# Products that nothing reads, put in TensorE's waits at three places, and a first stage that begins with its values

## The chip, the core and the metric

The kernel runs on one core of one Trainium2 chip. The metric is the device time of one execution in microseconds (us). Engines are named PE (TensorE), ACT (ScalarE), DVE (VectorE), POOL (GpSimd) and SP (SyncE, which here only issues transfers).

## What is computed

Two blocks over x, 2048 tokens by 512 features, in float32:

```
xn = layernorm(x)
x  = x + attention(xn) + experts(xn)         # softmax attention, 16 heads of 32, alibi and causal mask;
                                             # one of two experts for each token (512 -> 1024 -> 512)
xn = layernorm(x)
x  = x + linear_attention(xn) + glu(xn)      # lightning_attn in chunks of 128 with a decay for each head, then
                                             #   o * sigmoid(gate), a norm over each head, and @ Wo
                                             # _bitlinear with ternary weights: sigmoid(x w1) * (x w2), then w3

# attention: qkv = xn @ Wqkv + bqkv; softmax(q k / sqrt(32) + bias) v @ Wo + bo
# the norm over a head: og * rsqrt(mean(og * og) + EPS) * norm_w
```

## The kernel before

The program is a row of stages, each a block in which every engine has its own list of instructions: `normed_qkv_stage`, `attention_stage`, `projection_stage`, `experts_stage`, `lightning_stage`, `glu_stage`. Between two stages all engines meet (L58). Inside a stage the order on an engine is the order of the code, and semaphores (`wait_ge`, `then_inc`) are all that ties the engines together. TensorE takes a wait in order: what stands behind it in its list waits too.

Products of float32 quality are made of three passes (`three_passes`, L280 to L284): each operand is split into a rounded part (`h`, a copy on ACT, `WeightSplit.hi` at L155 for weights) and a rest (`l`, a subtraction, for weights on POOL, `WeightSplit.lo` at L169, for activations on DVE). So one 128 x 512 tile of a projection is 4 x 3 = 12 matmuls of 512 columns.

**The first stage** (`normed_qkv_stage`, L405) takes 4 chunks of 512 tokens, each of 4 tiles `t` of 128. `TokenNorm` (L302) works on a chunk in this order: statistics of the four tiles on DVE (L324, L327), one square root on ACT (L333), a short chain of five operations on 128x4 elements on DVE that ends in 1/sqrt (`rsqrt_newton`, L288, counted by the semaphore `newton`), four normalising passes on DVE (L343), 16 transposes on PE (`turn`, L352), four roundings on ACT (`high`, L358) and four rests on DVE (`low`, L362). `turn` writes its bank `k` with the features `k` of all tokens, so that a rounding needs all four tiles. Then PE makes 12 tiles of products for a chunk: four of queries, four of keys, four of values, `m` from 0 to 11. In chunk 0 ACT issues the 12 loads of weight pieces (queries first, then keys, then values); DVE computes the routing's dot products of chunk 0 (`gates`, L557) before it takes the first result. Later chunks are prepared while the one before is multiplied, at steps named `STATS_AT` and the like.

**The projection** (`projection_stage`, L1219) opens with `widen(0)`: eight products that spread the inverse softmax sums over the heads' rows, for which PE waits on loads and on two reciprocals on DVE (L1344). DVE scales two halves of the attention's output by them (L1332), ACT rounds, DVE takes the rest (L1337), and then come the products (L282 to L284) with `w.woh` and `w.wol`.

**The linear attention** (`lightning_stage`) opens with the same norm chain on chunk 0, then `first_turn` (16 transposes, L2025), roundings on ACT (L2206), rests on DVE (L2303) and the products of the values. Its tail, behind the last chunk, is `spread_inverses(3)` (L2041), four normalising passes on DVE (L2286), four roundings on ACT (L2195), four rests on DVE (L2290), and `output(3)`, four tiles of products.

`widen` and the three places at which the change adds products are in these lines:

```
            pe.wait_ge(spread_in, 16)
            widen(0)
...
            pe.wait_ge(ident_in, 16)
            first_turn()
...
            spread_inverses(NCH - 1)
            output(NCH - 1)
```

## Time and profile before

| | us |
|---|---|
| runs | 1640.88, 1642.31, 1651.42 (median 1642.31) |
| the profiled execution: its time / its span | 1642.89 / 1641.1 |
| TensorE busy | 1542.0 (94%) |
| VectorE busy | 999.8 (61%) |
| GpSimd busy | 641.7 (39%) |
| ScalarE busy | 593.5 (36%) |
| first stage / attention | to 162 / to 771 |
| projection and experts / linear attention / last feed-forward | to 1072 / to 1396 / to 1641 |

The span runs from the first to the last instruction of the trace; the time of an execution has 1.8 us more around it. The granted clock of TensorE is its share of 2.4 GHz in a stretch: 1.00 is 2.4 GHz and 0.50 is 1.2 GHz. A matmul's duration overlaps with the next one's, so what a matmul costs is the distance from one start to the next.

### The profile page before, as it was taken

The numbers are of one execution on the slowest core, as the hardware profiler recorded it, in microseconds if no ns is written. First come the engines' busy times: TensorE is split into PE (matmuls) and PEld (weight loads), VectorE is DVE, ScalarE is ACT, GpSimd is POOL, SyncE is SP. The second block draws the span as 40 slices with busy tenths as digits, with TensorE's granted clock in tenths as the row PEclk, the third lists the DMA queues.
The fourth block names the chain that finished last, engine by engine and source line by source line (L and its number), as shares of the span: only waits on it lengthen the run. The fifth ranks groups of instructions, "written<-read, shape, count | busy, mean of one in ns | idle before, by whom it ended". The sixth has DMA issues, their size and how long they took to land. (4 is left out here: it accounts for less than half of the span.)

```text
span 1641.1 us, 22085 instructions
## 1 busy us (share of the span) xinstructions
PE 1542.0 (94%) x7906; PEld 1076.4 (66%) x7906; DVE 999.8 (61%) x1719; ACT 593.5 (36%) x1125; POOL 641.7 (39%) x534
## 2 busy tenths in 40 slices
PE   5999989999999999997988999969999998999998
PEld 4887545454545545543667888857777776888887
DVE  7774887887878788873545655555464455232332
ACT  3121245555545555555212222254423231222221
POOL 4100277858868786700327677633020201000000
PEclk9999799999999999999899999989999999999999
DMA  6877544544526464301762222163030231420210
GB/s 237 248 256 202 128 132 117 118 108 141 121 63 171 119 135 99 108 15 33 247 215 65 65 77 72 46 204 113 1 129 1 78 93 50 148 103 1 103 52 26
DMA packets 104443, 182.07 MB, mean 111 GB/s; under 512 B 28712, under 2 KB 45224, under 8 KB 103684
## 3 DMA queue, kind: packets, MB, share of 16 engines
q1 hardware_dynamic: 87176, 119.20, 25.2%
q0 software_dynamic: 13520, 53.85, 11.1%
q10 hardware_dynamic: 3640, 7.61, 1.3%
q8 instruction: 65, 1.06, 0.3%
q14 instruction: 42, 0.34, 0.1%
HBM read 118.62 MB, written 61.74 MB: 110 GB/s over the span
## 5 line engine op out<-in xcount | busy, mean ns | idle before, releaser
L1072 ACT ACTIVATE att_probs<-att_ring 128x512 f32<-128x512 f32 (+3 forms) x640 | 298.2, 536 | 283.5 <-DVE att_ring L1103 145.8
L1094 DVE TENSOR_REDUCE att_maxes<-att_ring 128x2 f32<-128x1024 f32 (+7 forms) x366 | 339.2, 948 | 66.3 <-PE att_ring L992 55.4
L1025 PE MATMUL att_outp<-att_probs,att_vs 128*64 128x512 f32 (+3 forms) x1280 | 271.1, 545 | 0.4 <-ACT att_att L1056 0.4
L1025 PEld LDWEIGHTS att_outp<-att_probs,att_vs 128*64 128x64 f32 x1280 | 78.3, 137 | 120.0 <-issue 68.8
L1804 DVE TENSOR_TENSOR glu_hid<-glu_sig,glu_u 128x512 f32<-128x512 f32 x44 | 30.3, 688 | 140.6 <-PE glu_u L1744 140.6
L1013 PE MATMUL att_ring<-route_wah,route_wbh 102*128 102x512 f32 (+2 forms) x320 | 105.4, 403 | 6.4 <-DVE att_maxes L1094 5.2
L992 PE MATMUL att_ring<-route_wbh,route_wah 100*128 100x512 f32 (+2 forms) x320 | 102.8, 405 | 6.9 <-DVE att_maxes L1094 4.4
L1013 PE MATMUL att_ring<-moew_wal,moew_wbl 102*128 102x512 f32 (+2 forms) x320 | 101.1, 398 | 5.2 <-DVE att_maxes L1094 5.1
L992 PE MATMUL att_ring<-moew_wbl,moew_wal 100*128 100x512 f32 (+2 forms) x320 | 96.6, 378 | 3.8 <-DVE att_maxes L1094 2.3
L1013 PEld LDWEIGHTS att_ring<-route_wah,route_wbh 102*128 102x128 f32 x320 | 54.9, 191 | 68.6 <-issue 39.1
L2413 POOL TENSOR_TENSOR lin_sig<-lin_o_copy,lin_sig 128x512 f32<-128x512 f32 x16 | 20.4, 1277 | 198.5 <-ACT lin_o_copy L2266 198.5
L1013 PEld LDWEIGHTS att_ring<-moew_wal,moew_wbl 102*128 102x128 f32 x320 | 53.6, 188 | 65.4 <-issue 31.7
L1817 POOL DMA_DIRECT2D out<-glu_y x3 | 2.4, 802 | 217.3 <-DVE glu_y L1788 217.3
L1103 DVE TENSOR_TENSOR att_ring<-att_ring,route_cst 128x128 f32<-128x128 f32 x256 | 63.4, 292 | 32.5 <-PE att_ring L1013 32.0
L992 PEld LDWEIGHTS att_ring<-route_wbh,route_wah 100*128 100x128 f32 x320 | 62.9, 204 | 26.3 <-DVE att_maxes L1094 9.2
L992 PEld LDWEIGHTS att_ring<-moew_wbl,moew_wal 100*128 100x128 f32 x320 | 59.5, 189 | 20.4 <-ACT att_probs L1072 6.2
L1613 POOL TENSOR_SCALAR moe_r<-moe_z,route_f 128x512 f32<-128x512 f32 x34 | 68.6, 2022 | 3.9 <-DVE moe_z L1538 2.6
L1743 PE MATMUL glu_u<-tail_xh,tail_up 128*128 128x512 f32 x176 | 68.6, 390 | 1.3 <-DVEq L1796 1.3
L1756 PE MATMUL glu_down<-glu_w,glu_hh 128*128 128x512 f32 x176 | 68.6, 390 | 0.4 <-DVE glu_hl L1806 0.4
L1744 PE MATMUL glu_u<-tail_xl,tail_up 128*128 128x512 f32 x176 | 68.5, 389 | 0.0
L1757 PE MATMUL glu_down<-glu_w,glu_hl 128*128 128x512 f32 x176 | 68.5, 389 | 0.0
L1743 PE MATMUL glu_u<-glu_xh,tail_up 128*128 128x512 f32 x176 | 68.5, 389 | 0.0
(294 smaller groups left out, 3451.0 us busy)
## 6 DMA issues: line engine op xcount, KB each, us to landing
att_q_raw<-in_w POOLq DMA_DIRECT2D x48, 352.0 KB, 4.0
w_ternary<-att_q_out POOLq DMA_DIRECT2D x24, 352.0 KB, 2.7
tail_up<-w_ternary SPq DMA_DIRECT2D x22, 256.0 KB, 4.6
xn<-qkv_x SPq DMA_DIRECT2D x4, 1024.0 KB, 7.4
q_hi<-qkv_hi SPq DMA_DIRECT2D x16, 256.0 KB, 3.7
q_lo<-qkv_lo SPq DMA_DIRECT2D x16, 256.0 KB, 4.5
k_hi<-qkv_hi SPq DMA_DIRECT2D x16, 256.0 KB, 2.9
k_lo<-qkv_lo SPq DMA_DIRECT2D x16, 256.0 KB, 3.9
```

The source lines that it names most:

```text
L992: last = pe.matmul(out[h][:, 0:cover], qs[par][0:SROWS, h, t * P:(t + 1) * P], ks[par][0:SROWS, h, g * CH:g * CH + cover], start=True, sto ...
L1013: last = pe.matmul(out[h][:, start:CH], ks[par][:, h, kt * P:(kt + 1) * P], qs[par][:, h, c * CH + start:(c + 1) * CH], start=True, stop=True)
L1025: last = pe.matmul(outp[v_cols(h), off:CH], vs[p % 2][:, kt, v_cols(h)], probs[:, g % 4, h, off:CH], start=kt == 0, stop=kt == TT * (c + 1 ...
L1072: act.activation(probs[:, g % 4, h, off:CH], ring[:, rg.banks["score", g][h], off:CH], ACT.Exp).then_inc(exped, 1)
L1094: last = dve.tensor_reduce(maxes[:, hs, t, g:g + 1], banks[:, :, 0:width], AX.X, ALU.max)
L1103: dve.tensor_tensor(block, block, neg_k, ALU.add).then_inc(masked, 1)
L1613: pool.tensor_scalar(r[:, half, :], z[:, half, :], 0.0, rt.f1[:, j:j + 1], ALU.max, ALU.mult).then_inc(relued, 1)
L1743: pe.matmul(u[:, n % 2, :], w[:, f, k, :], xh[c % 2][:, k, :], start=k == 0, stop=False)
L1744: last = pe.matmul(u[:, n % 2, :], w[:, f, k, :], xl[c % 2][:, k, :], start=False, stop=k == KT - 1)
L1756: pe.matmul(down[:, t, :], hh[:, n % 2, s], w3[:, f, :], start=f == 0, stop=False)
L1757: last = pe.matmul(down[:, t, :], hl[:, n % 2, s], w3[:, f, :], start=False, stop=f == GT - 1)
L1804: dve.tensor_tensor(hid[:, n % 2, :], sig[:, n % 2, :], u2[:, n % 2, :], ALU.mult).then_inc(hid_ready, 1)
```

## The change

- A helper `keep_warm` issues `n` matmuls of 512 columns whose result nothing reads. It stands in TensorE's list at three places: 18 before and 6 behind `widen(0)` of the projection, 28 before `first_turn` of the linear attention, and 16 behind the last `spread_inverses`, before the last `output`. They wait for nothing, except the 16, which wait for `o` to be read (`o_taken`).
- In the first stage chunk 0 makes its values first, then queries and keys (`FIRST`). Its transposes go to a bank for each tile instead of each feature block, so that roundings, rests and the value products go tile by tile (`part`, `rows`, `xl_ready` counted one by one).
- The value weights are loaded first, on ACT's queue; the other eight pieces go to SP's queue, behind x and the constants. ACT first runs a square root on one element (`warm`).
- GpSimd waits for the first norm's short chain (`newton`) before its first rest of a weight.
- On DVE the routing's dot products are spread one to a step; two casts of constants come behind chunk 0. The second chunk's statistics, norm, transposes and roundings of chunk 0's loop get steps of their own. On SP the load of chunk `c + 2` comes behind the stores of the queries.
- `ranks` and `places` in the attention wait for both of their ring's banks instead of the first.

The core of the diff:

```diff
+def keep_warm(pe, out, wh, xh, n):
+
+    for _ in range(n):
+        pe.matmul(out, wh, xh, start=True, stop=True)
...
-                ins = pe.transpose(self.out[:, k, t * P:(t + 1) * P], self.x[c % 2][:, t, k * P:(k + 1) * P], self.ident)
-                if t == TT - 1:
+                to = (t, k) if c == 0 else (k, t)
+                ins = pe.transpose(self.out[:, to[0], to[1] * P:(to[1] + 1) * P], self.x[c % 2][:, t, k * P:(k + 1) * P], self.ident)
+                if k == KT - 1 if c == 0 else t == TT - 1:
                     ins.then_inc(self.turned, 1)
...
+    def rows(self, c, i):
+        return self.out[:, i, :].rearrange("p (k n) -> p k n", n=P) if c == 0 else self.out[:, i, :]
+
+    def high(self, act, c, i):
+        act.wait_ge(self.turned, c * KT + i + 1)
+        act.activation(self.part(self.xh[c % 2], c, i), self.rows(c, i), ACT.Copy).then_inc(self.xh_ready, 1)
+
+    def low(self, dve, c, i):
+        dve.wait_ge(self.xh_ready, c * KT + i + 1)
+        dve.tensor_tensor(self.part(self.xl[c % 2], c, i), self.rows(c, i),
+                          self.part(self.xh[c % 2], c, i).bitcast(F32), ALU.subtract).then_inc(self.xl_ready, 1)
...
+    FIRST = [*range(NQK, NP), *range(NQK)]
+    STATS_FIRST, NORM_FIRST, TURN_FIRST, HIGH_FIRST, LOW_FIRST = 2, 4, 6, 3, 7
...
-        ws = WeightSplit(st, D, [(w_d[k * P:(k + 1) * P, s], wh[:, k, s], wl[:, k, s]) for s, k in thirds[:2 * KT]]
-                         + [(w_d[k * P:(k + 1) * P, s], carried.h[:, k, :], carried.l[:, k, :]) for s, k in thirds[2 * KT:]],
-                         len(thirds))
+        ws = WeightSplit(st, D, [(w_d[k * P:(k + 1) * P, s], carried.h[:, k, :], carried.l[:, k, :]) for s, k in thirds[2 * KT:]]
+                         + [(w_d[k * P:(k + 1) * P, s], wh[:, k, s], wl[:, k, s]) for s, k in thirds[:2 * KT]], len(thirds))
...
+            for j in range(KT, len(ws.pieces)):
+                ws.load(sp, j)
...
-                if c + 2 < NCH:
-                    load_x(c + 2)
                 for m in range(NQK):
+                    if m == KT and c + 2 < NCH:
+                        load_x(c + 2)
...
-                pe.wait_ge(norm.xl_ready, (c + 1) * KT)
-                for m in range(NP):
-                    n = c * NP + m
-                    if c == 0 and m % KT == 0:
-                        ws.wait(pe, m + KT)
+                if c:
+                    pe.wait_ge(norm.xl_ready, (c + 1) * KT)
+                for i, m in enumerate(FIRST if c == 0 else range(NP)):
+                    n = c * NP + i
+                    if c == 0 and i < TT:
+                        pe.wait_ge(norm.xl_ready, i + 1)
+                    if c == 0 and i % KT == 0:
+                        ws.wait(pe, i + KT)
                     if n >= 4:
...
-                    if c + 1 < NCH and m == TURN_AT:
+                    if c + 1 < NCH and i == (TURN_AT if c else TURN_FIRST):
                         norm.turn(pe, c + 1)
...
-            ws.load_all(act)
             act.wait_ge(eps_set, 1)
-            ws.hi(act, 0)
-            ws.hi(act, 1)
+            act.activation(warm[:], eps[:], ACT.Sqrt)
+            for j in range(KT):
+                ws.load(act, j)
             norm.take_root(act, 0)
-            ws.hi(act, 2)
-            ws.hi(act, 3)
+            for j in range(KT):
+                ws.hi(act, j)
             xn_high(0)
             for j in range(KT, len(ws.pieces)):
                 ws.hi(act, j)
+            norm.take_root(act, 1)
             for c in range(NCH):
                 for m in range(NQK):
...
+            for i, m in enumerate(FIRST):
+                dve.wait_ge(made, i + 1)
+                if i < TT:
+                    value(0, i)
+                else:
+                    whole(0, m)
+                if i == STATS_FIRST:
+                    norm.stats(dve, 1, chunk_in(1))
+                if i == NORM_FIRST:
+                    norm.normalize(dve, 1)
+                if LOW_FIRST <= i < LOW_FIRST + KT:
+                    norm.low(dve, 1, i - LOW_FIRST)
+                if i == NP - 1:
+                    low(NQK - 1)
+                if NORM_FIRST < i <= NORM_FIRST + TT:
+                    gate(i - NORM_FIRST - 1)
             dve.wait_ge(ident_in, 16)
             for i, t in enumerate((early.ident, early.neg_q)):
                 dve.tensor_copy(t[:], early.cst[:, i, :]).then_inc(bf_ready, 1)
...
+            pool.wait_ge(norm.newton, norm.LINKS)
             ws.lo_all(pool)
...
                     if g == RANKS_AT:
-                        wait_freed(("ranks", 0), 0)
+                        for h in range(2):
+                            wait_freed(("ranks", 0), h)
                         router.ranks(pe)
                     if g == PLACES_AT:
-                        wait_freed(("places", 0), 0)
+                        for h in range(2):
+                            wait_freed(("places", 0), h)
                         router.sum_places(pe)
                     score(g)
...
+            keep_warm(pe, acc[:, 3, :], w.woh[:, 0, 0:P], w.woh[:, 1, :], 18)
             pe.wait_ge(spread_in, 16)
             widen(0)
+            keep_warm(pe, acc[:, 3, :], w.woh[:, 0, 0:P], w.woh[:, 1, :], 6)
             for n in range(NHC):
...
+            keep_warm(pe, o[:], carried.h[:, 0, 0:P], carried.h[:, 1, :], 28)
             pe.wait_ge(ident_in, 16)
             first_turn()
...
             spread_inverses(NCH - 1)
+            pe.wait_ge(o_taken, NCH * TT)
+            keep_warm(pe, o[:], wh["o"][:, 0, 0:P], wh["o"][:, 1, :], 16)
             output(NCH - 1)
```

ACT at the start of the first stage, its list before (the roundings of weights are L155, the square root is L333):

```order
L146 DMA qkv_wstage<-in_Wqkv 128x512 x12
L155 ACT_TABLE_LOAD
L155 ACTIVATE qkv_wh<-qkv_wstage 128x512 x2
L333 ACT_TABLE_LOAD
L333 ACTIVATE qkv_ln_root<-qkv_ln_mv,qkv_eps 128x4
L155 ACTIVATE qkv_wh<-qkv_wstage 128x512 x2
```

and now:

```order
L538 ACT_TABLE_LOAD
L538 ACTIVATE qkv_warm<-qkv_eps 128x1
L146 DMA qkv_wstage<-in_Wqkv 128x512 x4
L339 ACTIVATE qkv_ln_root<-qkv_ln_mv,qkv_eps 128x4
L155 ACTIVATE carried_h<-qkv_wstage 128x512 x4
```

The table for the square root is loaded ahead of the statistics, once; 4 loads instead of 12 stand ahead of it, and the pieces are those of the values (`carried_h`).

TensorE at the start of the projection, before:

```order
L1286 MATMUL proj_wide<-proj_inv,proj_spread 128x256 x4
L282 MATMUL proj_acc<-carried_h,proj_ath 128x512
L283 MATMUL proj_acc<-carried_l,proj_ath 128x512
L284 MATMUL proj_acc<-carried_h,proj_atl 128x512
```

and now:

```order
L283 MATMUL proj_acc<-carried_h 128x512 x18
L1332 MATMUL proj_wide<-proj_inv,proj_spread 128x256 x4
L283 MATMUL proj_acc<-carried_h 128x512 x6
L288 MATMUL proj_acc<-carried_h,proj_ath 128x512
L289 MATMUL proj_acc<-carried_l,proj_ath 128x512
L290 MATMUL proj_acc<-carried_h,proj_atl 128x512
```

The unread products stand on both sides of `widen(0)`; everything behind them in the list is as it was.

TensorE in the linear attention's tail, now:

```order
L2089 MATMUL lin_wide<-lin_inv,lin_cst 128x512 x4
L283 MATMUL lin_o<-lin_woh 128x512 x16
L288 MATMUL lin_ring<-lin_woh,tail_up 128x512
```

Before, the row in the middle was not there.

## Rows read from the trace of the kernel before

**Rows 1.** The page's busy line of TensorE (busy us, share of the span, instructions).

```profile
PE 1542.0 (94%) x7906; PEld 1076.4 (66%) x7906; DVE 999.8 (61%) x1719; ACT 593.5 (36%) x1125; POOL 641.7 (39%) x534
```

**Rows 2.** TensorE's waits (engine, line, waited for: us, times, longest).

```profile
PE qkv_turned L352 <- DVE qkv_x L343: 15.0, 1, 15.0
```

**Rows 3.** Timeline of the first stage (start, us, engine, line, operation, count, idle before).

```profile
8.56 0.69 DVE L324 BATCH_NORM_STATS2 qkv_ln_halves<-qkv_x 128x6 f32<-128x512 f32 x1 [0.65 <-DMA qkv_x<-in_x]
...
9.13 2.48 POOL L169 TENSOR_TENSOR qkv_wl<-qkv_wstage,qkv_wh 128x512 fp32r<-128x512 f32 x2 [8.70 <-ACT qkv_wh L155]
...
9.58 1.28 ACT L333 ACT_TABLE_LOAD   x1
...
11.87 1.19 DVE L298 TENSOR_SCALAR qkv_ln_tmp<-qkv_ln_tmp 128x4 f32<-128x4 f32 x1
...
14.31 1.92 DVE L343 TENSOR_SCALAR qkv_x<-qkv_x,qkv_ln_mv,qkv_ln_inv 128x512 f32<-128x512 f32 x4
...
21.21 0.79 PE L282 MATMUL qkv_acc<-route_wah,qkv_wh 128*128 128x512 f32 x1 [2.57 <-DVE route_wbh L362]
...
26.84 1.54 DVE L557 CUSTOM_DVE_ANT_0 qkv_product<-qkv_x,qkv_wg 128x512 f32<-128x512 f32 x1
...
27.35 0.44 PE L284 MATMUL qkv_acc<-route_wah,qkv_wl 128*128 128x512 f32 x1
...
43.92 0.68 DVE L557 CUSTOM_DVE_ANT_0 qkv_product<-qkv_x,qkv_wg 128x512 f32<-128x512 f32 x1
```

**Rows 4.** TensorE before the projection (window, us, busy, count, clock, DMA share, GB/s).

```profile
774.00:775.00 1.00, 0.00 (x0) 0.98 0.00 0
```

**Rows 5.** Timeline of the projection's start.

```profile
774.49 0.34 ACTq L1310 DMA_DIRECT2D proj_spread<-in_spread_heads  x1
...
779.40 3.37 DVE L1344 RECIPROCAL proj_inv<-proj_inv 128x256 f32<-128x256 f32 x2 [4.22 <-DMA proj_inv<-softmax_sums]
...
781.30 3.75 PE L1286 MATMUL proj_wide<-proj_inv,proj_spread 16*128 16x256 f32 x8 [10.29 <-DVE proj_inv L1344]
...
783.45 0.69 DVE L1332 TENSOR_TENSOR proj_at<-proj_at,proj_wide 128x512 f32<-128x512 f32 x1 [0.69 <-PE proj_wide L1286]
...
786.43 0.80 PE L282 MATMUL proj_acc<-carried_h,proj_ath 128*128 128x512 f32 x1 [1.38 <-DVE proj_atl L1337]
...
791.85 2.06 PE L1286 MATMUL proj_wide<-proj_inv,proj_spread 16*128 16x256 f32 x8
...
793.83 0.50 PE L282 MATMUL proj_acc<-carried_h,proj_ath 128*128 128x512 f32 x1
...
796.84 1.99 PE L1286 MATMUL proj_wide<-proj_inv,proj_spread 16*128 16x256 f32 x8
```

**Rows 6.** Timeline of the linear attention's start.

```profile
1076.52 1.28 ACT L2216 ACT_TABLE_LOAD   x1 [10.38 <-PEq L58]
...
1084.02 0.28 ACT L333 ACTIVATE lin_ln_root<-lin_ln_mv,lin_eps 128x4 f32<-128x4 f32 x1
...
1085.34 1.91 DVE L343 TENSOR_SCALAR tail_y<-tail_y,lin_ln_mv,lin_ln_inv 128x512 f32<-128x512 f32 x4
...
1086.03 3.37 PE L2025 MATMUL lin_wide<-lin_cst,tail_y 128*128 128x128 f32 x16 [13.70 <-DVE tail_y L343]
...
1087.78 0.69 DVE L2303 TENSOR_TENSOR tail_xl<-lin_wide,tail_xh 128x512 fp32r<-128x512 f32 x1 [0.53 <-ACT tail_xh L2206]
...
1089.15 0.47 PE L282 MATMUL lin_ring<-carried_h,tail_xh 128*128 128x512 f32 x1
```

**Rows 7.** Timeline of the linear attention's tail.

```profile
1375.06 1.14 PE L2041 MATMUL lin_wide<-lin_inv,lin_cst 32*128 32x512 f32 x8 [1.05 <-DVE lin_inv L299]
...
1381.45 0.79 PE L282 MATMUL lin_ring<-lin_woh,tail_up 128*128 128x512 f32 x1 [5.25 <-DVE lin_ogl L2290]
...
1385.88 0.43 PE L283 MATMUL lin_ring<-lin_wol,tail_up 128*128 128x512 f32 x1
```

**Rows 8.** TensorE in that tail (columns as in rows 4).

```profile
1379.00:1380.00 1.00, 0.00 (x0) 0.56 1.02 381
```

More of the change, by code:

```diff
@@ L562, in _ @@
             norm.normalize(dve, 0)
-            for k in range(KT):
-                norm.low(dve, 0, k)
+            for i in range(TT):
+                norm.low(dve, 0, i)
+            dve.wait_ge(wg_in, 16)
+            dve.tensor_tensor(wg[:, 0, :], wg[:, 0, :], wg[:, 1, :], ALU.subtract).then_inc(wg_ready, 1)
+            dve.wait_ge(wg_ready, 1)
+            dve.wait_ge(b_in, 32)
+            for i, m in enumerate(FIRST):
[14 more added lines that the diff above has]
+                    gate(i - NORM_FIRST - 1)
             dve.wait_ge(ident_in, 16)
@@ L567, in _ @@
                 dve.tensor_copy(t[:], early.cst[:, i, :]).then_inc(bf_ready, 1)
[L568 to L573 removed]
+            for c in range(1, NCH):
                 for m in range(NP):
```

76 lines of the change are left out of this document (34 added, 42 removed).

## The prediction

> **What bounds the kernel now.** I read the page first: TensorE is busy 94% of the span [rows 1], so the kernel is as long as TensorE's list plus the stretches in which TensorE stands still or runs at its lower clock. Next its waits: the longest single one is at the very start, 15.0 us until the first normalised tile [rows 2]. Then the timelines at the four places that the change touches, where "idle before" shows 10.29 us ahead of `widen(0)` [rows 5], 13.70 us ahead of the linear attention's transposes [rows 6] and 5.25 us ahead of the last output [rows 7]. The windows show what follows such a wait. TensorE ends the attention at 771.0, and its granted clock is 0.98 in the stretch from 774 and half behind it [rows 4]; in the tail it is idle from 1376.2 and the clock is 0.56 in the stretch from 1379, so half from about 1379.1 [rows 8]. The timeline gives the price: at 1.2 GHz the 12 matmuls of a tile take 791.85 - 786.43 = 5.42 us [rows 5], one each 0.43; at 2.4 GHz they take 796.84 - 793.83 = 3.01, one each 0.23 once they run. After each of these places TensorE runs without a gap worth counting, so what the place gives up moves everything behind it.
>
> **A, the first stage.** Before, ACT loads a table at 9.58 for the root that the statistics have just made possible, and DVE's normalising begins at 14.31 [rows 3]: 4.73 us. The same chain in the linear attention, with its table there already and GpSimd idle, goes from the root at 1084.02 to normalising at 1085.34, in 1.32 [rows 6]. The first stage pays the table (1.28) and about 2 us in short DVE operations held up beside GpSimd's rests: the one at 11.87 takes 1.19 us on 128x4 elements. The change takes the table load out and holds GpSimd back until the short chain is done: normalising begins at 9.58 + 1.32 = 10.9, 3.4 earlier. But now GpSimd starts just then, and its first four rests (2.48 for two, so 1.24 each) lie beside the four normalising passes. No row shows those passes beside GpSimd. The nearest is the routing's dot product: 1.54 beside GpSimd at 26.84 and 0.68 alone at 43.92 [rows 3], 0.86 more; the short operation lost 1.0. So the passes take 1.92 + 4 x 0.9 = 5.5 instead of 1.92 and end at 16.4. Behind them only the last tile's four transposes (a quarter of 3.37, 0.84 [rows 6]) and the first rest (0.69) stand, side by side, since the first product needs tile 0 alone: it starts at 17.2. The value weights' rests end at about 10.9 + 4 x 1.24 plus what the passes hold them up, 16 to 17, just in time. Before, the first product started at 21.21: **4.0 us gained**. The bounds: if each pass waits for one whole rest, a pair takes 1.24 + 0.48 and the start is at 10.9 + 6.9 + 0.8 = 18.6, a gain of 2.6. If they do not disturb each other the weights decide, at 15.9, a gain of 5.3; and if x arrives sooner, because ACT's queue has four loads ahead of the root instead of twelve, the statistics lose their waits on loads, three of about 0.6 (the last one 0.65 at 8.56), which makes 7.1. I take the row in between.
>
> Behind the start nothing should give it back. The products of chunk 0 are as many as before, and cold for some 6 us as before (21.21 to 27.35 [rows 3]). The query weights are due 12 x 4 matmuls later, over 11 us, which covers four roundings on ACT and four rests of at most 1.7. The dot products move from before the first result to beside later ones, 0.68 each, where a step of TensorE is 2.7 long; one step can have 0.74 + 0.68 + 0.69 + 0.68, about that length, and four accumulator banks absorb it. SP's load of a chunk waits one half loop longer and still has four steps. All this I cost at 0; if the cover fails, the second chunk's transposes are late next, by a step of DVE, 1 to 3 us. The second bank's wait at `ranks` and `places` is for results read two or more scores earlier: 0, at most 1 us.
>
> **B, the projection.** The 18 products start when the stage does, 774.5 (ACT's first transfer is at 774.49 [rows 5]), about where the clock falls. If it falls, they run cold until it rises; the stage itself needed 5.4 us of products for that (786.43 to 791.85). That is 13 products, and 5 warm ones take 1.2: done at 781.1, and `widen(0)` started at 781.30. So it is not held up. Warm, its eight products take 2.06 instead of 3.75 [rows 5], and DVE's scaling is no longer waited for by PE's half (783.45) but by the second reciprocal, 779.40 + 3.37 = 782.8; two scalings and a rest of 0.7 each end at 784.9, so the first product comes at 784.9 instead of 786.43: 1.5. The 6 products (1.4 us) fit into that wait. The first tile takes 3.0 instead of 5.4: 2.4. **3.9 us gained.** Bounds: 0 if the clock is down again when the tile starts; 4.5 if more of the scaling is brought forward.
>
> **C, the linear attention.** 28 products from about 1076.6 (ACT starts at 1076.52 [rows 6]): 5.4 us cold for 13, then 15 at 0.23, done at 1085.5, ahead of the transposes at 1086.03. These run warm, but they also wait for the last normalised tile at 1085.34 + 1.91 = 1087.25, and the first product waits for a rest that ends at 1087.78 + 0.69 = 1088.5, which ACT's earlier work sets. Before it started at 1089.15, warm already. **0.65 gained**, between -1 and 0.7.
>
> **D, the tail.** The 16 products start at 1376.2 behind `spread_inverses` and end at 1379.9; idle until the last rest at 1381.45 are 1.5 us instead of 5.25. The clock should stay. Before, the first ten distances took 1385.88 - 1381.45 = 4.43 [rows 7]; at 0.23 they take 2.3. **2.1 gained**, between 0 and 2.2. The 16 wait for `o_taken`, met long before.
>
> **The sum** is 4.0 + 3.9 + 0.65 + 2.1 = 10.6 us. The profiled execution took 1642.9, 0.6 above the median of the three runs (1642.3); from the median the forecast is 1631.7, so **1632 us**.
>
> **A rule weighed against this.** The 1.19 and 1.54 beside GpSimd show that the two engines hold each other up on some operations, and an excess of 0.9 to 1.0, less than a whole rest of 1.24, is what I used. The Trainium skill, "SBUF — State Buffer", section "Who interferes with whom", says that a VectorE instruction in a two-port mode, or with two inputs in SBUF, and a GpSimd instruction shut each other out for the whole instruction, so that which comes first decides. By this rule every pass can wait for a whole rest, which is the lower bound of A and the first rival.
>
> **The rivals.**
> 1. *GpSimd's rests take the place of the wait removed.* Released by the end of the short chain, they meet the normalising passes, each of which then waits a whole rest. For it: the rests are now due exactly there. Against it: an excess of 0.86 in the nearest row. A gives 2.6 or, with late value weights, less: 1633 to 1636, I say 1634. Chance 0.2.
> 2. *The start is freer than I think*: loads earlier and no mutual delay, A gives 6 to 7: 1629. Chance 0.13.
> 3. *The clock falls in spite of the products*, in the 1.5 us between the 16 and the last output, or between `widen(0)` and the first tile. For it: 1.14 us of `spread_inverses` did not hold the clock in the tail. D gives 0 and B 1.5 less: 1635 to 1638, I say 1636. Chance 0.12.
> 4. *The products stand in the way* (slower). TensorE's list is in order, so `widen(0)` waits for the 18 and the transposes for the 28. If the clock does not rise under them, 18 x 0.43 end at 782.2, 0.9 late, `widen(0)` stays cold and the 6 add 2.6 where 2.1 us of wait were: about 1.5 lost; the 28 end at 1088.6, 2.6 lost. With 4.1 lost here, nothing in D and A at 2.6 the sum is 1.5 to the bad: 1644. It decides from about 7 us of cold products on. Against it: every rise in the trace came within 6.2 us of dense work. Chance 0.03.
>
> The Trainium skill, "TensorE: Matmul & The Clock Gate", section "What's actually happening", says that the number of cold products before the rise differs from run to run of one kernel. This trace has 5.4 and 6.1 us, and in the linear attention 3.1 us of transposes (1086.03 to 1089.15) [rows 6]: that moves A's cold stretch by up to 1.5 us and the end of the 18 by as much.
>
> **From cases to numbers.** Forecast 0.5 (1630 to 1634), rivals 0.2, 0.13, 0.12, 0.03, and 0.02 for what I do not see. All gains at their upper bound make 7.1 + 4.5 + 0.7 + 2.2 + 1.5 = 16, against which nothing is likely to be complete: 1627 is the low end. Rival 3 with A at 2.6 makes 1637.5; with 1 us for the attention's waits, 1639 is the high end. A measurement of this kernel tells about 1%, 16.4 us, from no change: faster by more than that needs every upper bound, 0.04; slower by more needs something unforeseen, 0.02; within 1% 0.94.
>
> **What would show it.** In the trace after: no table load just ahead of the first root; normalising from about 10.9, its four passes longer than 1.92 together; the first product near 17. At the projection the first tile at 0.23 a matmul and `widen(0)` not later than before; clock 1.00 through the first tile. First products of the linear attention 12 us behind its stage's start instead of 12.6. In the tail the last output's first ten distances in 2.3. I am wrong if the first product starts after 19, if `widen(0)` or the transposes start at the end of unread products, or if the stages between, equal in their lists, change by more than 2 us.

## The result and the profile after

The changed kernel takes 1633.35 us, the median of 12 runs (1627.99 to 1640.89); the kernel before, beside it, 1644.68 us (12 runs, 1640.78 to 1651.42). The ratio is 0.9937, 95% interval 0.9922 to 0.9953: 11.3 us less by the medians, where 1632 was forecast. The profiled execution took 1632.59 us, its span is 1630.8 us against 1641.1.

The page's busy line of the changed kernel stands against [rows 1]:

```profile
PE 1555.3 (95%) x7974; PEld 1086.1 (67%) x7974; DVE 996.0 (61%) x1719; ACT 591.9 (36%) x1125; POOL 640.8 (39%) x534
```

TensorE is busy 13.3 us longer and yet the span is shorter. The 68 more instructions are the unread products, so busy time here is no measure of work: only the timelines tell what was won.

The span, cut at ten points that both kernels have, and the same cuts of a second trace of the changed kernel (the run `e11_changed_again` below), in us:

| stretch | before | forecast | after | again |
|---|---|---|---|---|
| start to first product | 21.2 | 17.2 | 18.2 | 17.5 |
| first product to the attention | 142.7 | 142.7 | 140.9 | 140.2 |
| attention | 610.6 | 610.6 | 609.6 | 609.9 |
| projection: start to second tile | 17.4 | 13.5 | 15.0 | 13.7 |
| rest of the projection | 59.0 | 59.0 | 58.7 | 60.6 |
| experts | 225.7 | 225.7 | 226.7 | 225.8 |
| linear attention: start to first product | 12.6 | 12.0 | 11.9 | 11.9 |
| its middle | 285.9 | 285.9 | 285.9 | 287.6 |
| its tail: inverses to the next block | 21.1 | 19.0 | 19.1 | 19.1 |
| the rest | 244.9 | 244.9 | 244.9 | 244.9 |

**First stage.** The timeline of the changed kernel (columns as in [rows 3], to which these rows answer; line 339 is the root, 349 the normalising passes, 359 the transposes, 169 a rest of a weight, 288 to 290 the three matmuls of a product), and then TensorE behind it:

```profile
0.72 1.28 ACT L538 ACT_TABLE_LOAD   x1 [0.72 <-PEq L2554]
...
9.20 0.69 DVE L330 BATCH_NORM_STATS2 qkv_ln_halves<-qkv_x 128x6 f32<-128x512 f32 x1 [0.66 <-DMA qkv_x<-in_x]
...
10.20 0.30 ACT L339 ACTIVATE qkv_ln_root<-qkv_ln_mv,qkv_eps 128x4 f32<-128x4 f32 x1 [7.98 <-DVE qkv_ln_mv L333]
...
11.54 5.82 DVE L349 TENSOR_SCALAR qkv_x<-qkv_x,qkv_ln_mv,qkv_ln_inv 128x512 f32<-128x512 f32 x4
11.59 5.49 POOL L169 TENSOR_TENSOR carried_l<-qkv_wstage,carried_h 128x512 fp32r<-128x512 f32 x4 [11.15 <-ACT carried_h L155]
...
13.28 1.09 PE L359 MATMUL qkv_turned<-route_cst,qkv_x 128*128 128x128 f32 x4 [13.28 <-DVE qkv_x L349]
...
17.41 1.11 PE L359 MATMUL qkv_turned<-route_cst,qkv_x 128*128 128x128 f32 x4 [0.29 <-DVE qkv_x L349]
```

```profile
18.18 0.77 PE L288 MATMUL qkv_acc<-carried_h,route_wah 128*128 128x512 f32 x1
...
20.88 0.41 PE L288 MATMUL qkv_acc<-carried_h,route_wah 128*128 128x512 f32 x1
```

The table load stands at 0.72, in nobody's way. The short chain takes from 10.53 to 11.54, 1.0 us. Then the four passes take 5.82 us where they took 1.92, ending some 1.4 us apart, side by side with the four rests, 1.37 each. The transposes follow pass by pass instead of all at once. The products are at full speed from 20.88: 2.7 us of cold products, where there were 6.1 [rows 3].

**Projection**, against [rows 5] (line 283 is an unread product, 1332 `widen`):

```profile
768.68 5.82 PE L283 MATMUL proj_acc<-carried_h 128*128 128x512 f32 x18 [3.53 <-PEq L58]
775.83 1.96 PE L1332 MATMUL proj_wide<-proj_inv,proj_spread 16*128 16x256 f32 x8 [1.33 <-DVE proj_inv L1392]
777.72 2.16 PE L283 MATMUL proj_acc<-carried_h 128*128 128x512 f32 x6
779.68 0.63 PE L288 MATMUL proj_acc<-carried_h,proj_ath 128*128 128x512 f32 x1
...
782.16 0.39 PE L288 MATMUL proj_acc<-carried_h,proj_ath 128*128 128x512 f32 x1
...
783.65 1.99 PE L1332 MATMUL proj_wide<-proj_inv,proj_spread 16*128 16x256 f32 x8
```

TensorE in the two microseconds around the first tile's start (window, us; then busy us and count of PE, PEld, DVE, ACT and POOL; then clock, DMA share, GB/s):

```profile
778.00:779.00 1.00, 1.00 (x5) 0.77 (x5) 0.98 (x2) 0.96 (x2) 0.00 (x0) 0.83 1.00 344
779.00:780.00 1.00, 1.00 (x4) 0.78 (x3) 0.91 (x2) 0.19 (x1) 0.00 (x0) 0.50 1.08 426
```

`widen(0)` takes 1.96 us instead of 3.75: the clock was up. Then it falls, at about 778.7, under the six unread products. Of the tile's twelve products the first five are followed by the next one 0.43 us later (a clock of 0.50), the sixth by 0.35, the others by 0.23.

**Linear attention**, its start against [rows 6]:

```profile
1068.96 1.28 ACT L2267 ACT_TABLE_LOAD   x1 [10.41 <-PEq L58]
...
1069.00 8.09 PE L283 MATMUL lin_o<-carried_h 128*128 128x512 f32 x28 [4.25 <-PEq L58]
...
1078.48 1.94 PE L2073 MATMUL lin_wide<-lin_cst,tail_y 128*128 128x128 f32 x16 [1.40 <-DVE tail_y L349]
...
1080.90 0.50 PE L288 MATMUL lin_ring<-carried_h,tail_xh 128*128 128x512 f32 x1 [0.47 <-DVE tail_xl L2354]
```

and its tail against [rows 7]:

```profile
1366.80 1.14 PE L2089 MATMUL lin_wide<-lin_inv,lin_cst 32*128 32x512 f32 x8 [1.05 <-DVE lin_inv L305]
...
1367.87 3.94 PE L283 MATMUL lin_o<-lin_woh 128*128 128x512 f32 x16
...
1373.19 0.50 PE L288 MATMUL lin_ring<-lin_woh,tail_up 128*128 128x512 f32 x1 [1.38 <-DVE lin_ogl L2341]
```

The 28 end 1.4 us before the transposes, the 16 end 1.38 us before the last output, and that output is warm from its first product. The granted clock over that tail, the third number from the end (columns as in the window lines above):

```profile
1366.00:1377.00 11.00, 8.82 (x40) 6.36 (x41) 7.71 (x13) 2.50 (x4) 0.00 (x0) 1.00 0.25 95
```

It is 1.00 where it fell to 0.56 in [rows 8].

### The profile page after: what moved, and what is told of

It is laid out like the page before. It is cut to its first block and busy times, and to the rows that moved or that the text cites. A ratio compares the mean times of both kernels' runs of the same rounds, so it can differ in the third digit from the quotient of the medians.

```text
span 1630.8 us, 22220 instructions
## 1 busy us (share of the span) xinstructions
PE 1555.3 (95%) x7974; PEld 1086.1 (67%) x7974; DVE 996.0 (61%) x1719; ACT 591.9 (36%) x1125; POOL 640.8 (39%) x534
```

## The experiments

Each run is held against runs of the kernel before on the same chip. The stretches that an edit leaves alone differ from trace to trace all the same: over the fourteen traces of this case the attention took 605.2 to 614.0 us with the same real products in it. A comparison of medians is therefore coarse (the 95% intervals below are 0.4% to 0.9% wide, 7 to 14 us), a trace tells the stretch in which an edit stands, and the verdicts below go by stretches.

### The two halves apart

`e1_products_only` is the kernel before with the unread products alone (the diff of `keep_warm` and its four calls); `e2_stage_only` is the changed kernel without them:

```diff
-            keep_warm(pe, acc[:, 3, :], w.woh[:, 0, 0:P], w.woh[:, 1, :], 18)
-            keep_warm(pe, acc[:, 3, :], w.woh[:, 0, 0:P], w.woh[:, 1, :], 6)
-            keep_warm(pe, o[:], carried.h[:, 0, 0:P], carried.h[:, 1, :], 28)
-            pe.wait_ge(o_taken, NCH * TT)
-            keep_warm(pe, o[:], wh["o"][:, 0, 0:P], wh["o"][:, 1, :], 16)
```

> The kernel before with only the unread products added, at the three places (18 and 6, 28, 16); the first stage is as before. My theory: each place works by itself. Against the kernel before: the first tile of the projection takes 3.0 to 4.0 us instead of 5.42, the first product of the linear attention comes 12.0 us behind its stage's start instead of 12.63, the last output 2.0 us sooner; in all 5 to 6.5 us less, ratio 0.996 to 0.997. Rival, that nearly all of the gain is the first stage's: ratio 0.999 or more. Rival, that the first stage hides it: ratio 0.994 as with the whole change.

> The change without any unread product. My theory: first product at 18.2 us instead of 21.2, its stage 4 to 5 us shorter in all, and nothing else; the projection's first tile takes 5.4 us again, the linear attention's first product comes 12.6 us behind the stage's start and the last output's first ten distances take 4.4 us. Ratio 0.997. Rival, that the first stage does nothing behind its own start: ratio 0.999 or more.

The products alone: 1640.59 us, ratio 0.9952 (0.9931 to 0.9974). The stage alone: 1638.57 us, ratio 0.9957 (0.9932 to 0.9983). The product of the two is 0.9909, the whole 0.9937 (0.9922 to 0.9953); with these intervals they may add up, and nothing shows that one half feeds the other. In the traces each gain stands where its half is: the first product at 21.2 and 17.5; the linear attention's start 11.9 and 12.8; its last stretch 19.1 and 21.9. Both intervals hold the ratios expected, 0.996 to 0.997 and 0.997. With the stage alone the first tile of the projection took 4.8 us instead of 5.4, with nothing changed there. The projection to its second tile took 16.3 us with the products alone, 1.1 less than before and 1.3 more than in the changed kernel, with the same 18 and 6. TensorE there:

```profile
774.95 4.36 PE L283 MATMUL proj_acc<-carried_h 128*128 128x512 f32 x18 [3.51 <-PEq L58]
781.84 2.28 PE L1292 MATMUL proj_wide<-proj_inv,proj_spread 16*128 16x256 f32 x8 [2.53 <-DVE proj_inv L1352]
...
786.77 0.63 PE L288 MATMUL proj_acc<-carried_h,proj_ath 128*128 128x512 f32 x1
```

The 18 ran at full speed, 4.36 us, and left 2.53 us of idle; `widen(0)` was partly cold and so were eight products of the tile, which took 4.4 us where 3.0 to 4.0 was expected.

### Where GpSimd's rests go

`e3_no_hold` lets GpSimd start as before, as soon as a weight is rounded; `e4_hold_longer` holds it until all four passes are over:

```diff
 e3   -            pool.wait_ge(norm.newton, norm.LINKS)
 e4   -            pool.wait_ge(norm.newton, norm.LINKS)
 e4   +            pool.wait_ge(norm.normed, TT)
```

> The change with GpSimd's wait for the short norm chain taken out, so that its rests begin as soon as ACT has rounded the first value weight (10.9 us). If holding GpSimd back matters as I reckoned, the short chain, which now takes 1.0 us from 10.53, meets one or two rests and loses 1 to 2 us, and the first product comes at 19.2 to 20 instead of 18.2. If the chain is over before it can be hit (ACT rounds only behind the root), nothing moves: 18.2 within 0.5.

> The change with GpSimd held until all four normalising passes are done instead of until the short chain is. If the passes are long because of GpSimd's rests, their 5.82 us fall to 1.92 and they end at 13.5; the rests then run from 13.5 and, no longer stretched, take 5.0 instead of 5.49, so the value weights are ready at 18.5 and the first product comes at 18.5 to 18.8, 0.3 to 0.6 later than now. If the passes are long for another reason (the tiles in use by a store, the load of chunk 1), they stay above 4 us and the first product comes at 22 or later.

Measured: 1634.65 us, 0.9922 (0.9898 to 0.9947), and 1635.85 us, 0.9935 (0.9909 to 0.9960): no difference from the whole change. The timelines of the first stage, of `e3` and then of `e4`:

```profile
10.81 5.12 POOL L169 TENSOR_TENSOR carried_l<-qkv_wstage,carried_h 128x512 fp32r<-128x512 f32 x4 [10.38 <-ACT carried_h L155]
10.84 1.25 DVE L304 TENSOR_SCALAR qkv_ln_tmp<-qkv_ln_tmp 128x4 f32<-128x4 f32 x1
...
13.35 3.77 DVE L349 TENSOR_SCALAR qkv_x<-qkv_x,qkv_ln_mv,qkv_ln_inv 128x512 f32<-128x512 f32 x4
```

```profile
10.87 1.92 DVE L349 TENSOR_SCALAR qkv_x<-qkv_x,qkv_ln_mv,qkv_ln_inv 128x512 f32<-128x512 f32 x4
...
12.87 5.42 POOL L169 TENSOR_TENSOR carried_l<-qkv_wstage,carried_h 128x512 fp32r<-128x512 f32 x4 [12.44 <-DVE qkv_x L349]
...
18.43 0.77 PE L288 MATMUL qkv_acc<-carried_h,route_wah 128*128 128x512 f32 x1 [3.23 <-POOL carried_l L169]
```

Without the hold, the meeting is only shifted: two operations of the short chain take 1.25 and 1.18 instead of 0.17 and 0.16, the passes, beside which fewer rests are left, 3.77. The first product is at 18.7. With the longer hold chain and passes are free (1.92), the rests of x come at 13.31 to 16.6, beside the weights' rests and at 0.69 each undisturbed; but the rests of the value weights end at 18.29, and TensorE waits 3.23 us for them. First product 18.4, in the range expected. x lands at another time in each run, so the fair measure is from the last statistics (9.20 in the changed kernel, 8.90, 8.53; 8.53 in its repeat) to the first product: 9.0 us in the changed kernel and in its repeat, 9.8 in `e3`, 9.9 in `e4`, 12.7 before. So the hold as the change has it is worth 0.9 us against none (less than the 1 to 2 expected), and more of it nothing: in `e3` and in the changed kernel TensorE's transposes come last, behind the passes, in `e4` GpSimd's 5.42 us. The price was shifted among them.

### Taking the bound apart

`e5_piece_waits` is `e4` with TensorE waiting for the value weights piece by piece in its first tile. `e6_early_rests` adds two roundings before the root, whose rests GpSimd makes at once:

```diff
 e5   +                        if n == 0:
 e5   +                            ws.wait(pe, k + 1)
 e6   +            ws.hi(act, 0)
 e6   +            ws.hi(act, 1)
              norm.take_root(act, 0)
 e6   -            for j in range(KT):
 e6   -                ws.hi(act, j)
 e6   +            ws.hi(act, 2)
 e6   +            ws.hi(act, 3)
 e6   +            for j in range(2):
 e6   +                ws.lo(pool, j)
              pool.wait_ge(norm.normed, TT)
 e6   +            for j in range(2, len(ws.pieces)):
 e6   +                ws.lo(pool, j)
```

> In the kernel of the run before (GpSimd held until all four normalising passes are over) TensorE waited for the rests of all the value weights, 18.3 us, before its first product. Here its first tile waits for them piece by piece, four pieces. Theory 1 (the wait for the whole is what sets the first product): the pieces are done at about 14.2, 15.6, 16.9 and 18.3 us, the first product is at about 15.3 us, where the transposes free it, instead of 18.4, and the stage ends 2 to 3 us sooner. Rival (the last piece sets the end of the first tile all the same): the first product is sooner, but the first tile ends less than 1 us sooner, and so does the stage.

> As the run with the waits piece by piece, and ScalarE rounds two of the four value pieces before the square root, and GpSimd makes their rests at once; only the other two wait for the normalising passes. Theory: the first two rests fall before the short chain, the last is done at about 15.6 us, and the first product is at about 15.2 us, bound by the transposes; the stage ends up to 1 us sooner than in the run with the piece waits alone. Rival (VectorE and GpSimd get in each other's way again): the early rests, 1.3 us each, stretch the short chain and the statistics by 1 to 2 us, and the passes, the transposes and the first product come that much later, so that the time is the same or up to 1 us worse.

TensorE in the first stage of `e5`, then GpSimd and TensorE in that of `e6`:

```profile
14.91 0.78 PE L288 MATMUL qkv_acc<-carried_h,route_wah 128*128 128x512 f32 x1
...
18.43 0.50 PE L288 MATMUL qkv_acc<-carried_h,route_wah 128*128 128x512 f32 x1 [0.58 <-POOL carried_l L169]
```

```profile
5.11 2.61 POOL L169 TENSOR_TENSOR carried_l<-qkv_wstage,carried_h 128x512 fp32r<-128x512 f32 x2 [4.68 <-ACT carried_h L155]
...
15.04 0.78 PE L288 MATMUL qkv_acc<-carried_h,route_wah 128*128 128x512 f32 x1
```

`e5`: first product at 14.9, 6.3 us behind the last statistics where it was 9.9 in `e4`, and the attention starts at 156.9 instead of 160.4: the theory, by half a microsecond more than expected. The last piece still costs 0.58 us of wait at 18.43. `e6`: that wait is gone, the attention starts at 155.3, 1.6 us earlier again, where up to 1 was expected. The wait is 0.6 of it; another 0.7 is a wait of TensorE for a later chunk's rests on VectorE, which stands at 86.9 in `e5` and not in `e6`, and which neither edit touches. Its early rests lie at 5.11 to 7.72, where VectorE waits for x, and neither the statistics nor the short chain are longer for them, so the rival is refuted. The medians, 1630.37 (0.9930, 0.9904 to 0.9956) and 1630.38 (0.9915, 0.9890 to 0.9941), don't tell the two apart: the attention of `e6` took 612.7 us, that of `e5` 606.4.

### A warm first tile

`e7_warm_first` is `e6` with 8 unread products of float32 (16 instructions in the trace) from 1.5 us on:

```diff
+            dve.memset(product[:], 1.0).then_inc(filled, 1)
...
+            pe.wait_ge(filled, 1)
+            keep_warm(pe, acc[:, 3, :], product[:, 0:P], product[:], 8)
```

> As the run with the early rests, and TensorE runs 8 unread products of 512 float32 columns in its first wait, before any input has been turned. Theory (what the first tile lacks is the clock): the granted clock is 1.00 from the first transposes, the cold stretch of 2.7 us in the first tile goes, and the stage ends 1.5 to 2 us sooner than in the run before this one. Rival (VectorE sets the pace, as it normalises and turns the halves): the transposes stay where they are and TensorE waits warm; the gain is under 0.5 us. Second rival: the clock falls again before the first transposes, and nothing is gained.

```profile
1.48 9.97 PE L283 MATMUL qkv_acc<-qkv_product 128*128 128x512 f32 x16 [1.48 <-DVE qkv_product L602]
11.50 1.94 PE L359 MATMUL qkv_turned<-route_cst,qkv_x 128*128 128x128 f32 x16
13.55 0.50 PE L288 MATMUL qkv_acc<-carried_h,route_wah 128*128 128x512 f32 x1
```

The transposes are warm, 1.94 us for the sixteen against 3.65 in the kernel before and 3.64 in `e6`, the first product is at 13.55, and nothing of the first tile is cold. The attention starts at 154.2, 1.1 us earlier than in `e6`: between theory and rival. A wait of 0.8 us at 84.1 for a later chunk's rests, which `e6` does not have, takes back what is missing of the theory's 1.5 to 2. It is luck that the unread products end at 11.45, just before the transposes: one more, two instructions at 0.43 us, would have held them up by 0.8 us. Median 1629.59 us, 0.9908 (0.9885 to 0.9932).

### Twice as many products

`e9_doubled` is the changed kernel with 36, 12, 56 and 32 for 18, 6, 28 and 16.

```diff
-            keep_warm(pe, acc[:, 3, :], w.woh[:, 0, 0:P], w.woh[:, 1, :], 18)
+            keep_warm(pe, acc[:, 3, :], w.woh[:, 0, 0:P], w.woh[:, 1, :], 36)
...
-            keep_warm(pe, o[:], carried.h[:, 0, 0:P], carried.h[:, 1, :], 28)
+            keep_warm(pe, o[:], carried.h[:, 0, 0:P], carried.h[:, 1, :], 56)
```

> The changed kernel with twice the unread products at four of its places: 36 for 18 and 12 for 6 at the start of the output projection, 56 for 28 at the start and 32 for 16 in the tail of the linear attention. Theory (in the changed kernel they end before what TensorE waits for, and one more costs 0.23 us once that cover is used up): the 36 end about 2.9 us after the attention's last result is there, the 56 about 5 us after the normalised states, the 32 about 2.3 us after the logits, and the kernel is about 10 to 13 us slower than the changed kernel, part of it given back by the clock. Rival (the waits are as long as ever and the places in the list don't bind): within 2 us of the changed kernel.

TensorE at the projection, at the linear attention's start and in its tail:

```profile
764.04 8.42 PE L283 MATMUL proj_acc<-carried_h 128*128 128x512 f32 x36 [3.53 <-PEq L58]
772.39 1.99 PE L1332 MATMUL proj_wide<-proj_inv,proj_spread 16*128 16x256 f32 x8
```

```profile
1066.59 14.31 PE L283 MATMUL lin_o<-carried_h 128*128 128x512 f32 x56 [4.25 <-PEq L58]
1080.73 1.91 PE L2073 MATMUL lin_wide<-lin_cst,tail_y 128*128 128x128 f32 x16
```

```profile
1371.07 7.55 PE L283 MATMUL lin_o<-lin_woh 128*128 128x512 f32 x32
1378.46 0.39 PE L288 MATMUL lin_ring<-lin_woh,tail_up 128*128 128x512 f32 x1
```

At all four places what follows starts when the products end: the list's order is real, and rival 4 of the prediction is a true mechanism beyond the counts chosen. The costs against the changed kernel are 1.1 us at the projection (16.1 for 15.0), 4.3 in the linear attention's start (16.2 for 11.9) and 2.1 in the tail (8.5 for 6.4), 7.4 in sum where 10 to 13 was expected; against the repeat of the changed kernel the projection's part is 2.4, and the sum 8.8. At the projection it is little because the clock did not fall at all there: 36 products in 8.42 us, and the tile warm. One run, 1637.81 us, span 5.2 us above the changed kernel's, with 4.4 us less in the attention.

### Filling more of the waits

`e10_projection_24` is `e7` with 24 and 9 for the 18 and 6. `e8_all_waits` is `e7` with 20 and 8, and further products where the trace shows a fall: 4, 12, 4 and 13 behind the first stage, the attention, the projection and the experts, 6 and 10 in the experts' first waits.

```diff
 e10  +            keep_warm(pe, acc[:, 3, :], w.woh[:, 0, 0:P], w.woh[:, 1, :], 24)
 e10  +            keep_warm(pe, acc[:, 3, :], w.woh[:, 0, 0:P], w.woh[:, 1, :], 9)
 ...
 e8   +            keep_warm(pe, ring[:, 0, :], w.woh[:, 0, 0:P], w.woh[:, 1, :], 12)
 ...
 e8   +            keep_warm(pe, up[:, 0, :], w.wah[:, 0, 0:P], w.wah[:, 0, 0:CH], 13)
```

> As the run with 8 products before the first transposes, and more unread products: 20 for 18 and 8 for 6 at the start of the output projection, 4 behind the first stage, 12 behind the attention, 4 behind the projection, 13 behind the experts, and 6 and 10 in the experts' first waits. Theory (the clock falls behind each wait in which TensorE is idle, and a filled wait keeps it): no stretch at a granted clock of 0.5 at 764 to 772, at 840 to 848, at 856 to 864 and at the start of the linear attention; the first tile of the projection runs in 3.0 us, the experts start about 1 us and end about 2 us sooner; 3 to 5 us less than the run with the 8 products alone. Rival (those stretches wait for VectorE, ScalarE or a transfer, and the clock is no part of their time): the clock stays up and the time stays within 1 us. Second rival: products stand in the way of the list where the waits are shorter than thought, 1 to 2 us slower.

> As the run with 8 products before the first transposes, and 24 for 18 and 9 for 6 unread products at the start of the output projection alone. Theory (the first tile of the projection was cold in the changed kernel because 1.3 us without work stood before the spreading products, and those use 16 of 128 rows): the 24 end 7.2 us after the attention's last result, where the spreading products began in any case, the clock does not fall before or in the first tile, and the stretch from the attention's end to the second tile is 13.9 us instead of the changed kernel's 15.0. Rival (the run with 36 and 12 held the clock only by its 12 products right before the tile): the clock falls as before, and the stretch is 14.5 to 15.5 us. In the total this is within the scatter of the runs: the trace decides.

TensorE at the projection's start in `e10`, and between the experts and the linear attention in `e8`:

```profile
761.85 7.33 PE L283 MATMUL proj_acc<-carried_h 128*128 128x512 f32 x24 [3.52 <-PEq L58]
...
771.03 2.35 PE L283 MATMUL proj_acc<-carried_h 128*128 128x512 f32 x9
773.22 0.40 PE L288 MATMUL proj_acc<-carried_h,proj_ath 128*128 128x512 f32 x1
```

```profile
1060.85 6.63 PE L283 MATMUL lin_o<-carried_h 128*128 128x512 f32 x28 [1.30 <-PEq L58]
1070.33 3.09 PE L2090 MATMUL lin_wide<-lin_cst,tail_y 128*128 128x128 f32 x16 [2.85 <-DVE tail_y L349]
1073.07 0.78 PE L288 MATMUL lin_ring<-carried_h,tail_xh 128*128 128x512 f32 x1
```

`e10`: no idle before `widen(0)` and a warm tile, as the theory has it; but the 9 products end only at 773.2, behind the tile's inputs, so the stretch is 14.3 us, not 13.9. `e8`: the falls at 764 to 772 and 856 to 864 are gone, the one at 838.8 to 842.2 stays, and the one in the linear attention has moved: the 28 run warm (6.63 us), leave 2.85 us of idle, and now the transposes and the first products are cold, 12.3 us for the stretch instead of 11.9. Medians 1625.96 us (0.9898, 0.9855 to 0.9941) and, with the two counts alone, 1625.62 us (0.9880, 0.9849 to 0.9911), on one chip: the 49 products in other waits bring nothing that can be measured. Nor is a gain of 24 and 9 over 18 and 6 shown: the interval of `e7` (0.9885 to 0.9932) overlaps both, and its own stretch, 13.8 us, is shorter than the 14.3 of `e10`.

### The changed kernel again, beside the best one

> The changed kernel once more, unaltered, on the same chip as the next run. Theory (how long the first tile of the projection runs at half the clock is a matter of when the clock happens to fall, since the same 18 and 6 products gave 15.0 us from the attention's end to the second tile in the changed kernel and 13.3 to 14.4 in four kernels that differ from it in the first stage alone): the stretch comes out anywhere from 13.3 to 15.0 us, and the rest as in the first trace, within 0.3 us. Rival (the first stage's order, which the four have changed, sets it in some way): 15.0 us again. The time is 0.992 to 0.996 of the kernel before.

> The kernel with waits piece by piece, early rests, 8 products before the first transposes and 24 and 9 at the projection once more, beside the changed kernel. Theory: the first products at 13.6 us and the first tile warm again, 14.3 us from the attention's end to the second tile; 4 to 8 us (0.25% to 0.5%) less than the changed kernel beside it. Rival (its lead is the scatter between chips): within 3 us of the changed kernel.

TensorE at the projection's start in the repeat of the changed kernel:

```profile
767.66 6.93 PE L283 MATMUL proj_acc<-carried_h 128*128 128x512 f32 x18 [3.52 <-PEq L58]
774.84 1.96 PE L1332 MATMUL proj_wide<-proj_inv,proj_spread 16*128 16x256 f32 x8 [0.24 <-DVE proj_inv L1392]
776.73 1.66 PE L283 MATMUL proj_acc<-carried_h 128*128 128x512 f32 x6
778.30 0.50 PE L288 MATMUL proj_acc<-carried_h,proj_ath 128*128 128x512 f32 x1
```

The same instructions as in the first trace; this time the 18 took 6.93 us, there was 0.24 us of idle, and the tile was warm throughout: 13.7 us. Not all of the rest was within 0.3 us: the clock was down from 797.1 to 800.5 in the middle of the projection, a place where it had stayed up before (60.6 for 58.7), and the linear attention's middle took 287.6 for 285.9. Times: the changed kernel 1635.28 us (11 runs, 0.9939, 0.9918 to 0.9961), the kernel with 24 and 9 beside it 1628.93 us (6 runs, 0.9891, 0.9856 to 0.9927). Between those two the ratio of the means is 0.9954, 0.993 to 0.998 by resampling their runs: the version that the experiments led to beats both kernels, the changed one by 6.4 us in the medians. The theory said 4 to 8. Its own repeat of the projection's stretch is 14.0 us, not shorter than the 13.7 beside it. The lead stands at the start: its attention begins at 154.2, the changed kernel's at 157.7.

## Why the prediction was right, and where not

**The sum** was 10.6 us; spans differ by 10.3, medians by 11.3. By terms it is closer in the total than in its parts, and part of that is luck: in the first trace A and B gave 2.5 us too little, and a term put at 0 gave 1.8. The time, 1632 for 1633.35, was counted from 1642.3, the median of three runs of the kernel before; the twelve gave 1644.68.

| term | forecast | after | again |
|---|---|---|---|
| A, start | 4.0 | 3.0 | 3.7 |
| rest of the first stage | 0 | 1.8 | 2.5 |
| B | 3.9 | 2.35 | 3.7 |
| C | 0.65 | 0.69 | 0.70 |
| D | 2.1 | 2.0 | 2.1 |
| stretches with the same list | 0 | 0.4 | -2.7 |

The prediction named a change of more than 2 us in the stages with equal lists as a sign of being wrong. The repeat's -2.7 and the attention's 605.2 to 614.0 us pass it: that sign was drawn narrower than the scatter of one kernel.

**A, the start.** The chain is as forecast but for its input: the last statistics start at 9.20 instead of 8.56 [rows 3], since the last piece of x landed later, and normalising at 11.54 instead of 10.9. In the repeat they start at 8.53 and 10.88, and the first product at 17.5, 0.3 from the forecast. At equal inputs the gain is 12.7 - 9.0 = 3.7. The passes took 5.82 us where 5.5 was taken from the dot product's row: 1.45 each. The Trainium skill, "SBUF — State Buffer", section "Who interferes with whom", has the two engines shut each other out for the whole instruction; by this case's durations, 0.48 and 1.24, that is an estimated 1.72 a pair and 6.9 us in all. The trace agrees in part: taken one by one, the first rest runs its 1.26 us as if alone and the first pass, begun 0.05 us before it, takes 1.60. But the other passes take 1.49 and start 1.41 us apart, 0.3 less than the rule gives, the rests beside them take 1.45, and the sum is 5.82. So rival 1 was the right mechanism at a smaller price, and most of it was in the sum already.

**The rest of the first stage** was put down as "cold for some 6 us as before". That was the step that failed: 2.7 us were cold. The 6.1 us held 14 products, the 2.7 hold 6; eight fewer at 0.43 instead of 0.23 make 1.6 of the 1.8 us. Four traces have the changed first stage word for word: with 3, 6, 7 and 10 cold products (the repeat, the first trace, `e2`, `e9`) the stretch took 140.2, 140.9, 141.1 and 141.7 us, 0.2 for each. So the cold products are the price of this term. How much of it the change earned is not shown: `e1`, with the first stage of before, had 8 of them, not 14 (and lost as much again in a wait of 1.35 us at 94.3). Before, TensorE stood idle 2.57 us between the transposes and the first product [rows 3], and now the transposes reach to 18.5, past the first product's start; but `e9` had no such idle either, and 10 cold products. The moved dot products, the load of a chunk and the wait for both banks cost nothing that shows.

**B, the projection.** The step "done at 781.1, the first tile takes 3.0" holds in the repeat and fails in the first trace. It was a sum over one course of the clock, and there are several. The traces with 18 and 6, in the order of how long the 18 took:

| run | the 18, us | idle behind | start to second tile |
|---|---|---|---|
| `e4` | 4.34 | 2.19 | 14.4 |
| `e1` | 4.36 | 2.53 | 16.3 |
| changed kernel | 5.82 | 1.33 | 15.0 |
| `e5` | 5.95 | 1.00 | 13.5 |
| `e3` | 6.92 | none | 13.3 |
| changed kernel again | 6.93 | 0.24 | 13.7 |
| `e7` | 6.93 | 0.35 | 13.8 |
| `e6` | 7.24 | none | 13.6 |

At the ends of the table the course is plain. When the clock falls early, the 18 take 6.9 to 7.2 us, next to no idle is left, and the tile is warm. When they run warm, in 4.3 to 4.4, they end early, over 2 us of idle follow, and the clock falls in front of the real products. In the middle it is not: the changed kernel and `e5` differ by 0.13 us in the 18 and 0.33 in the idle, and only the first had a second fall. What decides, the idle or the time since the last fall, the traces don't separate, and `e8`, with 1.74 us of idle behind 20 warm products and 8 more before a warm tile, speaks against the idle alone. The eight stretches have a mean of 14.2 us; 24 and 9 gave 14.3 and 14.0. The larger counts had a warm tile both times and no shorter mean, since the 9 themselves then stand before the tile.

The Trainium skill, "TensorE: Matmul & The Clock Gate", section "What's actually happening", says that the number of cold products differs from run to run of one kernel. The two traces of the changed kernel agree: of the same 18, 7 were cold in the one and 13 in the other. I had used it to move the end of the 18, and not to ask where the next fall would then be.

**C and D** came out to 0.1 us. In C the clock was never the price: the transposes ran in 1.94 instead of 3.37 [rows 6], and the first product still waited for the rest of x, as forecast. In D 1.38 us of idle behind the 16 did not bring the clock down. **Rival 3** is half true: the clock fell between `widen(0)` and the tile, not in the tail. (Its times, 1636 and 1637.5, are reckoned with 1.5 us for B, not with "1.5 less", which would give 1635.3 and 1636.7.) **Rival 2** (a free start) did not come: passes and rests did meet. **Rival 4** needs more products than there are, as `e9_doubled` shows. One argument against it was misread: that every rise came within 6.2 us of dense work. At the start of the attention before, the granted clock is 0.50 from 164.0 to 177.6, and TensorE is busy for 13.3 of the 14 us from 164 to 178 (one stretch of it, columns as in [rows 4]):

```profile
174.00:176.00 2.00, 2.00 (x7) 0.50 0.00 1
```

**What stays open**: why the clock falls at 797 in one trace and not in another of the same kernel. The fall came just behind a wait of 0.3 us for a rest on VectorE, and `e3` has both, a wait of 0.8 and the fall, at the same place; but `e5` and `e8` waited 0.4 and 0.5 there, and the clock stayed up. The first trace had no such wait. So it is not shown either where the repeat lost its 2.7 us, or whether the 0.0028 between the product of the halves' ratios and the whole's, some 4.6 us, is more than the intervals allow for by chance.

## What to carry to other kernels

Count unread products from the time that they take when they run at full speed as well as at half: a count that just fills the wait when cold leaves it open when warm, and the real work can then start cold. A count that fills it when warm stands in the way when cold: here 24 and 9 kept the tile warm twice in two traces and were no shorter on average than 18 and 6. When several engines meet at one moment, look for what waits for the whole of a batch: here splitting one wait into four (3.5 us) was worth more than holding GpSimd back from the batch beside it (0.9 us). And judge an edit of a few microseconds by its own stretch in several traces: the untouched stretches move as much as it does.

## What the runs showed that was not expected

- An operation of VectorE on 128x4 elements that begins 0.03 us behind a rest of GpSimd ends 0.03 us behind it: in `e3` it runs from 10.84 to 12.09, and the first of the four rests, taken by itself, from 10.81 to 12.07. It took 0.17 alone. The rest of x, with one input in PSUM and one in SBUF, took 0.69 us beside the weights' rests (`e4`) and with GpSimd idle [rows 6]. The Trainium skill, "SBUF — State Buffer", section "Who interferes with whom", says that a VectorE instruction with at most one SBUF input, outside the two-port modes, does not contend; this agrees.
- Unread products ahead of the first real work were free up to the end of the wait and made sixteen transposes take 1.94 us instead of 3.65 (`e7`).
- With the real products unchanged, the attention took from 605.2 to 614.0 us. The granted clock goes with it in part: it was at 0.50 for 17 us of the shortest and for 31 to 35 us of two that took 612.7 and 612.0, but for 25 us of the longest.
